# Causal self attention of a transformer decoder layer: batches of three units in place of two, and six slots of exponentials

## The reference

```python
scores = jnp.einsum('bhqd,bhkd->bhqk', q, k) / jnp.sqrt(jnp.asarray(hd, xq.dtype))
scores = scores + bias[None]        # relative bias and the causal mask
attn = jax.nn.softmax(scores, axis=-1)
out = jnp.einsum('bhqk,bhkd->bhqd', attn, v)
```

## Time and profile before

| what | us |
|---|---|
| median of three runs (lowest, highest) | 2820.68 (2820.12, 2822.91) |
| the profiled execution | 2827.99 |
| its span, first to last instruction | 2826.2 |
| TensorE busy in the span | 2717.2 |
| VectorE, ScalarE, GpSimd busy | 1599.9, 1237.4, 418.0 |

### The profile page before, as it was taken

The page is one execution under the profiler, slowest core; times in us unless marked ns, Lnnn a source line. Parts: engine busy times, 40 slices in busy tenths (PEclk is TensorE's granted clock), DMA queues, the critical chain, the costliest instruction groups (busy, mean ns, idle before and its releaser), DMA issues. The chain is left out here.

```text
span 2826.2 us, 40019 instructions
## 1 busy us (share of the span) xinstructions
PE 2717.2 (96%) x12704; PEld 1799.7 (64%) x12704; DVE 1599.9 (57%) x3850; ACT 1237.4 (44%) x2624; POOL 418.0 (15%) x497
## 2 busy tenths in 40 slices
PE   7999989999999999999999899889989999999998
PEld 6788854444444444444444477767768888888887
DVE  5554356777777777777777288467632222222221
ACT  2322113555555555555555443388833323332222
POOL 5000040000000000000000413088556000000000
PEclk9999978999999999999999999999999999999999
DMA  7656563222222222222221487555431000000000
GB/s 222 227 183 205 187 159 73 68 67 69 69 69 69 69 70 69 69 69 67 59 60 45 109 218 242 188 168 172 138 130 39 30 30 30 30 0 30 30 16 15
DMA packets 137813, 272.39 MB, mean 96 GB/s; under 512 B 24773, under 2 KB 54725, under 8 KB 132362
## 3 DMA queue, kind: packets, MB, share of 16 engines
q1 hardware_dynamic: 132394, 254.57, 31.3%
q0 software_dynamic: 5216, 15.33, 1.9%
HBM read 175.44 MB, written 99.98 MB: 97 GB/s over the span
## 5 line engine op out<-in xcount | busy, mean ns | idle before, releaser
L1204 ACT ACTIVATE sa_pr<-sa_st 128x512 f32<-128x512 f32 (+3 forms) x1280 | 610.5, 532 | 551.0 <-DVE sa_st L1264 310.3
L1170 PE MATMUL sa_ov<-sa_pr,sa_v 128*33 128x512 f32 (+3 forms) x2560 | 536.3, 540 | 0.0
L1250 DVE TENSOR_REDUCE sa_part<-sa_mp 128x1 f32<-128x512 f32 (+3 forms) x768 | 411.5, 581 | 113.5 <-PE sa_mp L1151 113.0
L1161 PE MATMUL sa_st<-sa_q,sa_k 97*128 97x512 f32 (+3 forms) x1280 | 441.8, 414 | 17.2 <-ACT sa_pr L1204 12.5
L1161 PEld LDWEIGHTS sa_st<-sa_q,sa_k 97*128 97x128 f32 x1280 | 217.1, 190 | 319.1 <-ACT sa_pr L1204 210.0
L1151 PE MATMUL sa_mp<-sa_k,sa_q 96*128 96x512 f32 (+3 forms) x1280 | 374.2, 387 | 10.4 <-DVE sa_mp L1225 5.2
L1247 DVE CUSTOM_DVE_ANT_0 sa_mp<-sa_mp,sa_ub 128x512 f32<-128x512 f32 (+3 forms) x512 | 317.3, 662 | 79.4 <-PE sa_mp L1151 75.1
L148 PE MATMUL ff_f<-sa_q,ff_w 128*128 128x512 f32 x1024 | 337.7, 391 | 3.2 <-DVE sa_k L271 3.2
L1900 PE MATMUL ff_o<-ff_w,ca_q 128*128 128x512 f32 x1280 | 330.0, 392 | 3.6 <-DVE ca_q L1953 3.6
L1953 DVE TENSOR_TENSOR ca_q<-ca_v,ca_q 128x512 fp32r<-128x512 f32 x128 | 95.3, 744 | 381.9 <-ACT ca_q L1936 381.9
L1170 PEld LDWEIGHTS sa_ov<-sa_pr,sa_v 128*33 128x33 f32 x2560 | 122.1, 111 | 256.6 <-issue 206.9
(11 more groups left out here) (216 smaller groups left out, 3258.9 us busy)
## 6 DMA issues: line engine op xcount, KB each, us to landing
sa_q<-scratch_q SPq DMA_DIRECT2D x96, 256.0 KB, 7.3
sa_k<-scratch_k SPq DMA_DIRECT2D x96, 256.0 KB, 8.5
scratch_q<-sao_qst SPq DMA_DIRECT2D x32, 512.0 KB, 4.6
ca_q<-scratch_q SPq DMA_DIRECT2D x32, 512.0 KB, 4.2
scratch_q<-sa_q SPq DMA_DIRECT2D x28, 512.0 KB, 8.1
scratch_k<-sa_q SPq DMA_DIRECT2D x28, 512.0 KB, 5.6
sa_v<-scratch_v SPq DMA_DIRECT2D x16, 528.0 KB, 12.6
scratch_o<-sa_osb SPq DMA_DIRECT2D x128, 66.0 KB
```

The costliest lines, as they stand in the source:

```text
L1161: pe.matmul(st[bank(u, h)][:, 0:w], ks[n.par][:, h, kb * P:(kb + 1) * P], qs[n.par][:, h, g * GW + c0:(g + 1) * GW], start=True, stop=True ...
L1170: last = pe.matmul(ov[64 * h:64 * h + VW, c0:GW], vs[n.par][:, kb, h, :], pr[:, u % 4, h, 0:GW - c0], start=(u in opens), stop=(u in ends))
L1204: act.activation(pr[:, u % 4, h, 0:w], st[bank(u, h)][:, 0:w], ACT.Exp, scale=SCALE).then_inc(s["exp"], 1)
L1250: dve.tensor_reduce(to, tile, AX_X, ALU.max).then_inc(s["red"], 1)
```

## The change

The batches are no longer pairs everywhere. A new table gives their sizes for each group: 2, 2 for the first, 3, 3, 2 for the second, 3, 3, 3, 3 for the third, and 3, 3, 2, 2, 2, 2, 2 for the fourth. That is 16 batches in a slot instead of 20; units 4 to 9, 12 to 23 and 24 to 29 are in batches of three. Each batch is worked as before: next to the j-th unit of the batch stand the scores of the j-th unit of the next batch and the max steps of this unit, with the values of the whole batch at the end. The tile `pr` has six slots instead of four, three for batches of even number and three for odd ones; a slot's exponential waits until the values of the batch before last are through. The order of units, the table of max steps by unit, the three banks of scores and the two double banks of the max steps stay as they are.

```diff
+SELF_BATCHES = ((2, 2), (3, 3, 2), (3, 3, 3, 3), (3, 3, 2, 2, 2, 2, 2))
@@
-    def after(n, u, left):
-
-        for v in (u + 2, u + 3):
-            if v < NU:
-                yield n, v
-            elif left:
-                yield n + 1, v - NU
+    batches = []
+    for size in itertools.chain(*SELF_BATCHES):
+        u = batches[-1][-1] + 1 if batches else 0
+        batches.append(list(range(u, u + size)))
...
+    MOST = max(len(b) for b in batches)
+
+    def after(n, i, left):
+
+        if i + 1 < len(batches):
+            return [(n, v) for v in batches[i + 1]]
+        return [(n + 1, v) for v in batches[0]] if left else []
+
+    def room(u):
+
+        i = next(i for i, b in enumerate(batches) if u in b)
+        return i % 2 * MOST + u - batches[i][0]
+
+    def gone(u):
+
+        i = next(i for i, b in enumerate(batches) if u in b)
+        return batches[i - 1][0] if i else batches[-1][0] - NU
@@
-        pr = k.sb(f"{name}_pr", [P, 4, 2, GW])
+        pr = k.sb(f"{name}_pr", [P, 2 * MOST, 2, GW])
@@
             def slot(n, left):
-                for u in range(0, NU, 2):
-                    ahead = list(after(n, u, left))
-                    for i in range(2):
-                        if ahead:
-                            scores(*ahead[i])
-                        for m, a in steps_at(n, u + i, left):
-                            max_step(m, a)
-                    values(n, u)
-                    values(n, u + 1)
+                for i, batch in enumerate(batches):
+                    ahead = after(n, i, left)
+                    for j in range(MOST):
+                        if j < len(ahead):
+                            scores(*ahead[j])
+                        if j < len(batch):
+                            for m, a in steps_at(n, batch[j], left):
+                                max_step(m, a)
+                    for u in batch:
+                        values(n, u)
@@
             def exponent(n, u):
                 w = GW - units[u][2]
-                waits(act, s["av"], NU * n + u - 2)
+                waits(act, s["av"], NU * n + gone(u) + 1)
...
-                    act.activation(pr[:, u % 4, h, 0:w], st[bank(u, h)][:, 0:w], ACT.Exp, scale=SCALE).then_inc(s["exp"], 1)
+                    act.activation(pr[:, room(u), h, 0:w], st[bank(u, h)][:, 0:w], ACT.Exp, scale=SCALE).then_inc(s["exp"], 1)
```

More of the change, by code:

```diff
@@ L983, in emptied @@
         return max(i for i in range(2 * NU) if i % NST == j) - 2 * NU
-    def after(n, u, left):
-        for v in (u + 2, u + 3):
-            if v < NU:
-                yield n, v
-            elif left:
-                yield n + 1, v - NU
+    batches = []
+    for size in itertools.chain(*SELF_BATCHES):
+        u = batches[-1][-1] + 1 if batches else 0
+        batches.append(list(range(u, u + size)))
+    assert batches[-1][-1] == NU - 1 and len(batches) % 2 == 0
+    assert all(u in [b[-1] for b in batches] for u in ends)
+    MOST = max(len(b) for b in batches)
[9 more added lines that the diff above has]
+        return batches[i - 1][0] if i else batches[-1][0] - NU
     def steps_at(n, u, left):
@@ L1170, in values @@
                     last = pe.matmul(ov[64 * h:64 * h + VW, c0:GW], vs[n.par][:, kb, h, :],
-                                     pr[:, u % 4, h, 0:GW - c0], start=(u in opens), stop=(u in ends))
+                                     pr[:, room(u), h, 0:GW - c0], start=(u in opens), stop=(u in ends))
                 last.then_inc(s["av"], 1)
@@ L1178, in _ @@
             pe.wait_ge(s["ones"], 3)
-            scores(Step(0, 0, UNROLL), 0)
-            scores(Step(0, 0, UNROLL), 1)
+            for u in batches[0]:
+                scores(Step(0, 0, UNROLL), u)
             def slot(n, left):
-                for u in range(0, NU, 2):
-                    ahead = list(after(n, u, left))
-                    for i in range(2):
-                        if ahead:
-                            scores(*ahead[i])
-                        for m, a in steps_at(n, u + i, left):
-                            max_step(m, a)
-                    values(n, u)
-                    values(n, u + 1)
+                for i, batch in enumerate(batches):
[8 more added lines that the diff above has]
+                        values(n, u)
             run(pe, N, slot, UNROLL)
@@ L1210, in empty @@
                 act.activation(osb[:, g % 2, :], ov[:], ACT.Copy).then_inc(s["out"], 1)
-            exponent(Step(0, 0, UNROLL), 0)
-            exponent(Step(0, 0, UNROLL), 1)
+            for u in batches[0]:
+                exponent(Step(0, 0, UNROLL), u)
             def slot(n, left):
-                for u in range(0, NU, 2):
-                    for m, v in after(n, u, left):
+                for i, batch in enumerate(batches):
+                    for m, v in after(n, i, left):
                         exponent(m, v)
-                    if u + 1 in ends:
-                        empty(n, u + 1)
+                    if batch[-1] in ends:
+                        empty(n, batch[-1])
             run(act, N, slot, UNROLL)
@@ L1269, in _ @@
             dve.memset(ov[:], 0.0).then_inc(s["init"], 1)
-            bias(Step(0, 0, UNROLL), 0)
-            bias(Step(0, 0, UNROLL), 1)
+            for u in batches[0]:
+                bias(Step(0, 0, UNROLL), u)
             def slot(n, left):
[L1274 to L1281, removed]
+                for i, batch in enumerate(batches):
+                    ahead = after(n, i, left)
+                    for j in range(MOST):
+                        if j < len(ahead):
+                            bias(*ahead[j])
+                        if j < len(batch):
+                            for m, a in steps_at(n, batch[j], left):
+                                reduce(m, a)
+                    if left == 0 and batch[0] == INVERSE_AT:
                         dve.wait_ge(s["sums"], 16)
```

## The result

Four executions of the changed kernel took 2902.50 to 2915.18 us, median 2908.57, against 2820.40 before (four, 2819.71 to 2822.91): the ratio is 1.031 (95% interval 1.0298 to 1.0322), 88 us slower, where 67 were forecast. The profiled execution is the fastest of the four, 2902.50 us, and by that one (2827.99 before) the difference is 74.5 us.

The account below looks back on a forecast made before the run. TensorE was taken to pace the slot, busy 49.28 of 49.64 us. With the saving included, 14 slots of +4.5 us and the two ends gave +67 us on the 2820.68 median: 2888 us, range 2850 to 2916.

Parts of the forecast that it names:

- Part 1, the saving: On TensorE, 64 fewer rounds of changing between kinds of matmul, 0.35 us each: -22 us.
- Part 2, the walk: Scores of unit 4 to unit 32: longer score phases wait for VectorE and ScalarE, +4.5 us a slot, saving included.
- M42: Sign, units 7 to 9: max step 42 starts 3.6 us behind unit 10's scores; before 3.0 the forecast is wrong.
- S26's heads: Sign, units 21 to 23: if the two heads of unit 26's scores start under 0.5 us apart, the forecast is wrong.
- the S weight loads: Sign on TensorE: idle time of score weight loads behind the exponentials grows by half or more.
- Part 3, the ends: First and last slots of the attention stage: about 2 us more each.
- The sum: Whole kernel: +67 us, giving 2895 us for the profiled execution and 2888 us for the median.
- the 14 slots times 4.5: Slots between the first and the last: 4.5 us more in each, 63 us in all.
- the banks are enough: Rival: only TensorE's work counts and the other engines keep up; -22 us, 2799 us; chance 0.06.
- the delay compounds: Rival: ScalarE is late for the values too, output evacuation delays exponentials; over +95 us, about 2925; chance 0.06.

Follow-up runs that it names:

- Experiment 3: Changed kernel, max steps left out and seven score banks instead of three: batches of three 2444.13 us; the same with pairs everywhere 2466.26 us.
- experiments 1 to 3: Changed kernel with pairs everywhere, 2823.12 us; with reductions, then exponentials too, cut short, in threes and pairs; without max steps and with seven score banks, threes 2444.13, pairs 2466.26.
- experiment 2: Changed kernel and its pairs version, reductions cut to 8 columns: 2808.71 and 2781.07 us; exponentials behind the first slot also cut to 64: 2751.40 and 2739.25 us.
- retabled kernel: Changed kernel with three max steps moved a unit earlier, so units 4 to 9 carry 1, 0, 2, 1, 1, 1: 2876.46 us, ratio 1.0186.
- evened table: Changed kernel with the max steps evened out over the batches of three, one a unit where it can be: 2900.21 us, ratio 1.0275.

## Why the prediction came out right

**Part 1, the saving, -22 us:** right. Experiment 3 measured 22.1 us, 0.34 a round in its stretch against 0.35. The agreement to the microsecond is luck in part: 0.35 was an estimate for a mixture of rounds, with max steps or scores ahead of the values, and the measurement is of rounds with scores alone. In the kernel itself the saving cannot be seen by itself.

**Part 2, the walk, +4.5 us a slot:** measured 5.0. Ten batches, walked and measured (medians over the slots): 4.10 and 4.09; 5.81 and 5.79; 6.78 and 6.92; 3.47 and 3.37; 6.13 and 6.47; 4.78 and 4.66; 6.08 and 6.25; 6.25 and 6.27; 6.01 and 6.08; 4.65 and 4.73. Sum 54.06 and 54.63. The walk chained start times from the old rows through two engines in order, and the waits stood where it put them: M42 at 3.63 (3.58 walked; 3.0 was the sign of being wrong), S26's heads 1.01 apart (0.5 was the sign). The largest miss is 0.34, in the batch of unit 12 (M0 to M4), for which the prediction shows no rows; its cause wasn't looked for. One sign failed, that on the S weight loads (above): as a measure of this wait the weight loads' idle time was the wrong row, since in pairs they stood idle too while matmuls ran over them.

**Part 3, the ends, +4:** the first slot rose by 1.5 (74.9 to 76.4), the last by 2.7 (46.9 to 49.6).

**The sum.** 88 was measured and 67 forecast. The term that was too small is the 14 slots times 4.5, 63 us: 14 times 5.0 is 70. A term was missing, the clock (below), 7 us in the profiled execution. 70 + 7 + 4 is 81, which is what the stage lost there, from its first matmul to its last V: it ended at 1605.7 us of the span before and at 1686.7 after. The program behind the stage was 6.5 us shorter, 1213.3 against 1219.8 us, and that isn't the change: in the twelve traces of kernels with max steps this same part takes between those two values, 1213.9 in pairs with six slots. The profiled execution before happens to be the slowest of them in this part, which fits its 7 us over the median, and the profiled one after the fastest. So in these two executions the change cost 81 us and not 74.5, and the remaining 7 of the 88 are not traced. The other three executions are 5 to 13 us slower still; their mean granted clock is 0.976 to 0.978 against 0.981, which fits more slots at half clock, but only one execution has a trace.

**The rivals.** That the banks are enough is out by experiments 1 to 3: the threes lose 88 us on three banks and gain 22 only where no score waits. That the delay compounds was near in amount (its bound was +95), but its mechanism is hardly seen: V's weight loads stood idle 2.9 us behind exponentials in the stretch, 1.8 before, and in the batch of units 7 to 9 V waits for no exponential. The Trainium skill (TensorEngine Tiling, PSUM Bottleneck) is more careful than the prediction made it: it says that tiling speeds up TensorE and not the emptying of PSUM, so that the copy may become the bottleneck. Here the trace agrees for the greater part. With what empties the banks cut short, first the reductions and then the exponentials, the lag of the threes shrinks from 88 to 27 and to 12 us.

**What the loss is made of.** The lag of the threes behind the pairs is +88 us as they are, +27 with short reductions, +12 with short exponentials too, -22 with no waits. So some 60 us go with the length of VectorE's reductions and 15 with that of the exponentials; both are shown. The last 34, between +12 and -22, are argued: that step takes the max steps away and adds banks in one, and the rows in experiment 2 show a wait on the way round three banks that short operations leave in place. The half clock is within the first part: with short reductions the trace has one such stretch in the stage behind the first slot, where the changed kernel has five.

## What to carry to other kernels

When an in-order producer is grouped into longer bursts to save switches, count the buffers between it and its consumers, not the mean load. VectorE was busy 75% of the time and still held up four of the ten walked batches by 0.5 to 1.7 us, as the ring of two or three buffers holds less than the burst. More slots at the far end of the chain (here six of exponentials in place of four) don't help if the near ones (three banks, two max buffers) stay. Walking one burst by start times from the old timeline gave the stretch's length to about 1%, single batches to 0.34 us; for a moved step it must count the step's own time where it goes, and who stands behind it on the second engine.

## What the runs showed of the hardware that was not expected

TensorE's clock fell to half after the wait in the batch of units 7 to 9, in five of the sixteen slots. Stretches of the changed kernel, a slot at full clock and one that fell (us, busy PE, PEld, DVE, ACT, POOL, granted clock, DMA):

```profile
921.60:925.80 4.20, 3.30 (x13) 1.75 (x11) 3.72 (x11) 1.35 (x4) 0.00 (x0) 1.00 1.03 214
925.80:930.00 4.20, 3.78 (x17) 1.47 (x17) 3.04 (x7) 0.87 (x2) 0.00 (x0) 1.00 1.01 247
1081.20:1085.40 4.20, 3.27 (x13) 1.75 (x11) 3.74 (x11) 1.35 (x4) 0.00 (x0) 1.00 1.04 210
1085.40:1089.60 4.20, 4.14 (x13) 1.24 (x13) 2.58 (x6) 0.00 (x0) 0.00 (x0) 0.59 1.01 247
```

```profile
1084.86 1.40 PE L1168 MATMUL sa_mp<-sa_k,sa_q 96*128 96x512 f32 x2 [0.73 <-DVE sa_part L1268]
...
1086.18 3.66 PE L1187 MATMUL sa_ov<-sa_pr,sa_v 128*33 128x256 f32 x12
```

Before the fall both slots look alike: TensorE idle for 0.73 or 0.74 us, M42's heads 0.6 apart. Then V's twelve matmuls take 3.66 us at 1.2 GHz for most of their time, against 2.35 at 2.4 GHz, and M42 to S12 4.92 us against 3.30. The batch takes 6.92 us at full clock and 8.23 to 8.53 in the five slots. A wait of TensorE can thus cost its own length and 1.3 to 1.6 us of half speed behind it, in some slots and not in others. The retabled kernel, without that wait, has one such stretch in the stage behind its first slot, at another place; the one with the evened table has twelve, eleven of them behind its 1.40 us wait. A wait of 0.74 us isn't needed, though: with one step moved, the longest idle time of TensorE in this batch is some 0.4 us (0.36 to 0.43), and the clock still fell there in three slots.
